# Row maxima of full attention: one transposition and one transfer for two slots, maxima four slots ahead instead of three

## The reference, cut to what matters

```python
s = jnp.einsum('bhtd,bhsd->bhts', q, k) / scale
m = jnp.max(s, axis=-1, keepdims=True)
e = jnp.exp(s - m)
num = jnp.einsum('bhts,bhsd->bhtd', e, v)
den = jnp.sum(e, axis=-1, keepdims=True) + EPS
out = (num / den).transpose(0, 2, 1, 3).reshape(B, T, H * D)
```

## Time and profile before

| what | us |
|---|---|
| median of 3 runs | 1204.31 (1196.77 to 1204.63) |
| the profiled execution | 1204.97 |
| its span, first to last instruction | 1203.2 |
| TensorE busy | 1051.9 (87%) |
| VectorE busy | 864.4 (72%) |
| ScalarE busy | 748.8 (62%) |
| mean granted TensorE clock | 0.932 |

### The profile page before, as it was taken

How to read it: one execution, slowest core, us unless ns; L and a number is a source line. 1 busy time by engine, 2 the same in 40 slices (tenths; PEclk the granted TensorE clock), 3 DMA queues, 4 the chain that set the end, 5 groups by cost and what they waited for, 6 DMA issues and landing times.

```text
span 1203.2 us, 31909 instructions
## 1 busy us (share of the span) xinstructions
PE 1051.9 (87%) x13025; PEld 484.6 (40%) x13025; DVE 864.4 (72%) x1151; ACT 748.8 (62%) x1510; POOL 90.4 (8%) x370
## 2 busy tenths in 40 slices
PE   7598999794587999899999998779898899999986
PEld 3344545442253333334444344442333334344443
DVE  3553654345554799899999944555999999999635
ACT  2422545237213389889999982231888899999921
POOL 8000100000000000000000000000000000000000
PEclk9897999888778999999999997789999999999978
DMA  3473432100006322220101000044313201001000
GB/s 96 138 211 72 98 92 74 39 1 1 0 0 189 86 64 63 55 51 18 29 19 24 24 20 10 1 124 140 71 44 72 53 18 25 22 18 30 18 15 35
DMA packets 73825, 64.97 MB, mean 54 GB/s; under 512 B 27792, under 2 KB 53648, under 8 KB 73552
## 3 DMA queue, kind: packets, MB, share of 16 engines
q1 hardware_dynamic: 73680, 62.94, 20.0%
HBM read 27.06 MB, written 35.85 MB: 52 GB/s over the span
## 4 chain that ended last, share of the span: by engine, by line
DVE 43%; PE 38%; DMA 7%; issue 4%; ACT 4%; SPq 3%; DVEq 0%; ACTq 0%
DVE nmf L1331 35%; PE wide L556 24%; PE bank L556 14%; DMA KQs<-m_dram 4%; ACT xcsq L949 2%; DVE xcsq L1148 1%; DVE res L1148 1%; SPq L378 1%; DVE nmt L1290 1%; ACT big L949 1%; SPq L309 1%; DVE big L1410 1%; SPq L299 1%; DVE x L1148 1%; DMA qf_dram<-big 1%
## 5 line engine op out<-in xcount | busy, mean ns | idle before, releaser
L1331 DVE TENSOR_REDUCE nmf<-wide 128x1 f32<-128x1024 f32 x512 | 587.3, 1204 | 40.4 <-PE wide L556 40.3
L949 ACT ACTIVATE big<-wide 128x512 f32<-128x512 f32 (+1 forms) x703 | 403.4, 601 | 81.1 <-PE wide L556 54.7
L556 PE MATMUL wide<-big,KQs 48*128 48x512 bf16 (+1 forms) x1376 | 349.4, 344 | 4.3 <-DVE nmf L1331 3.3
L556 PE MATMUL bank<-big,V 128*9 128x128 f32 x8192 | 319.9, 274 | 12.5
L556 PE MATMUL wide<-KQs,big 50*128 50x512 bf16 (+1 forms) x1035 | 266.9, 324 | 11.9 <-DMA KQs<-m_dram 10.8
L556 PEld LDWEIGHTS bank<-big,V 128*9 128x9 f32 x8192 | 176.8, 90 | 233.7 <-ACT big L949 221.7
L949 ACT ACTIVATE big<-bank 128x512 f32<-128x512 f32 (+2 forms) x473 | 233.8, 516 | 23.2 <-PE bank L556 10.6
L556 PE MATMUL bank<-KQs,big 50*128 50x512 bf16 x341 | 130.3, 382 | 6.8 <-DMA KQs<-m_dram 6.8
L556 PEld LDWEIGHTS wide<-KQs,big 50*128 50x128 bf16 x1035 | 70.6, 95 | 117.9 <-ACT big L949 56.5
L1296 DVE TENSOR_REDUCE nmw<-wide 95x4 f32<-95x512 f32 (+1 forms) x96 | 61.2, 640 | 58.9 <-PE wide L556 57.9
L949 ACT ACTIVATE xcsq<-xcsq 128x512 f32<-128x512 f32 x32 | 20.1, 630 | 124.2 <-DVE xcsq L1148 124.2
(11 more groups left out here) (175 smaller groups left out, 833.3 us busy)
## 6 DMA issues: line engine op xcount, KB each, us to landing
o_dram<-big SPq DMA_DIRECT2D x128, 64.0 KB
big<-kf_dram SPq DMA_DIRECT2D x32, 200.0 KB
kf_dram<-big SPq DMA_DIRECT2D x24, 256.0 KB, 4.2
qf_dram<-big SPq DMA_DIRECT2D x24, 256.0 KB, 4.0
KQs<-qf_dram SPq DMA_DIRECT2D x32, 192.0 KB
ow_dram<-scr SPq DMA_DIRECT2D x32, 142.5 KB
big<-kw_dram SPq DMA_DIRECT2D x16, 275.0 KB
kw_dram<-scr SPq DMA_DIRECT2D x12, 352.0 KB, 5.7
```

Of the source, the lines that this page charges most:

```text
L556: return nc.tensor.matmul(o, l, r, start=start, stop=stop, **kw)
L949: return nc.scalar.activation(o, i, f, **kw)
L1331: nc.vector.tensor_reduce(nmf[:, (s0 + i) % 4, c:c + 1], wide[:, k:k + 2, :].rearrange("p g c -> p (g c)"), AX.X, ALU.max, negate=True).th ...
```

## The change

`AHEAD` becomes 4. Slots are taken in pairs: GpSimd writes the split maxima of an even slot into columns 0 to 7 and those of the odd slot that follows into columns 8 to 15 of one `nms` buffer. VectorE transposes once per pair, after the first maximum of the slot that follows the pair. SyncE writes that block to `m_dram` once per pair and then issues two reads, one for each slot, right behind the wait for the write; it does this in even slots, for slots i + 2 and i + 3. `load_group(1)` is issued ahead of the first pair instead of after the first two slots. Windowed attention keeps its own order. `turned` itself and the semaphores stay; `nm_turned` and `nm_out` now count pairs in full attention.

```diff
--- before.py
+++ after.py
@@ -37,7 +37,7 @@
 ROW_PARTS = ((2, 1, 0, 1, 0, 0), (0, 1, 2, 0, 1, 0))
 GROUPS = 4
 SLOTS = 4 * H
-AHEAD = 3
+AHEAD = 4
 PTS = 8
 LAG = 4
 AHEAD_W = 5
@@ -68,7 +68,7 @@
         ow_dram = nc.dram_tensor("ow_dram", (B, H, 32, 4 * OW), F32).ap()
         qf_dram = nc.dram_tensor("qf_dram", (KR, H, N), BF16).ap()
         kf_dram = nc.dram_tensor("kf_dram", (KR + 2, H, N), BF16).ap()
-        m_dram = nc.dram_tensor("m_dram", (SLOTS, 32, P), BF16).ap()
+        m_dram = nc.dram_tensor("m_dram", (SLOTS // 2, 32, P), BF16).ap()
         o_dram = nc.dram_tensor("o_dram", (4, H, 4, 32, P), F32).ap()
 
         bank = [ctx.enter_context(nc.psum_tensor(f"bank{i}", [P, 512], F32)) for i in range(2)]
@@ -386,6 +386,7 @@
 
             def full_attention(layer):
                 s0 = UNITS + (layer - 1) * SLOTS
+                j0 = UNITS + (layer - 1) * SLOTS // 2
 
                 def load_group(g):
                     b, p0 = g // GROUPS, g % GROUPS * 2
@@ -404,12 +405,17 @@
                     sp.wait_ge(part_out[k], 96 * 2 * layer)
 
                 def shift(i):
-                    s = s0 + i
+                    s, j = s0 + i, j0 + i // 2
                     b, y, p, r, h = place(i)
-                    sp.wait_ge(nm_out[s % 4], 16 * (s // 4 + 1))
-                    at = S * b + 512 * y
+                    sp.wait_ge(nm_out[j % 4], 16 * (j // 4 + 1))
+                    at, o = S * b + 512 * y, 8 * (i % 2)
                     sp.dma_start(qop[r + KR:r + KR + 2, p, at:at + 512],
-                                 m_dram[i, 0:8, :].rearrange("(a c) q -> a (c q)", a=2)).then_inc(nm_in[s % 8], 16)
+                                 m_dram[i // 2, o:o + 8, :].rearrange("(a c) q -> a (c q)", a=2)).then_inc(nm_in[s % 8], 16)
+
+                def pair(i):
+                    turned(j0 + i // 2, m_dram[i // 2, :, :])
+                    shift(i)
+                    shift(i + 1)
 
                 def heads_out(i):
                     s = s0 + i
@@ -426,16 +432,11 @@
                     at = 512 * blk + P * c
                     sp.dma_start(aT[:, at:at + P], o_dram[blk, :, c, 0:D, :]).then_inc(o_in[blk], 16)
 
-                for i in range(AHEAD - 1):
-                    turned(s0 + i, m_dram[i, :, :])
-                    if i:
-                        shift(i - 1)
                 load_group(1)
+                pair(0)
                 for i in range(SLOTS):
-                    if i + AHEAD - 1 < SLOTS:
-                        turned(s0 + i + AHEAD - 1, m_dram[i + AHEAD - 1, :, :])
-                    if i + AHEAD - 2 < SLOTS:
-                        shift(i + AHEAD - 2)
+                    if i % 2 == 0 and i + 2 < SLOTS:
+                        pair(i + 2)
                     if i in LOADS:
                         load_group(LOADS[i])
                     if i:
@@ -528,11 +529,11 @@
                    [[-1, 8], [-8, H], [0, D]], 1)
             pool.drain().then_inc(moe_const, 1)
 
-            def split_shift(s, nm, rows):
+            def split_shift(s, nm, rows, j, at):
                 n = nm.shape[1]
-                first, second = nms[0:rows, s % 4, 0:n], nms[0:rows, s % 4, n:2 * n]
-                if s >= 4:
-                    pool.wait_ge(nm_turned, s - 3)
+                first, second = nms[0:rows, j % 4, at:at + n], nms[0:rows, j % 4, at + n:at + 2 * n]
+                if j >= 4:
+                    pool.wait_ge(nm_turned, j - 3)
                 pool.tensor_copy(first, nm).then_inc(nm_first, 1)
                 pool.wait_ge(nm_first, s + 1)
                 pool.tensor_tensor(second, nm, first, ALU.subtract).then_inc(nm_split, 1)
@@ -540,14 +541,14 @@
             if nst > 0:
                 for u in range(UNITS):
                     pool.wait_ge(wx_read, len(WG) * (u + 1))
-                    split_shift(u, nmw[0:QT, u % 4, :], QT)
+                    split_shift(u, nmw[0:QT, u % 4, :], QT, u, 0)
 
             for layer in (1, 2):
                 if nst > 2 * layer + 2:
                     for i in range(SLOTS):
                         n = (layer - 1) * SLOTS + i
                         pool.wait_ge(mx_read, 4 * (n + 1))
-                        split_shift(UNITS + n, nmf[:, n % 4, :], P)
+                        split_shift(UNITS + n, nmf[:, n % 4, :], P, UNITS + n // 2, 8 * (n % 2))
 
 
         @block.tensor
@@ -1283,11 +1284,11 @@
                 dve.wait_ge(g0, 5)
                 nc.vector.tensor_copy(q0o[:, :], bk(7)[:, 400:400 + B]).then_inc(g0v, 1)
 
-            def turn(s):
+            def turn(j, s):
                 dve.wait_ge(nm_split, s + 1)
-                if s >= 4:
-                    dve.wait_ge(nm_out[s % 4], 16 * (s // 4))
-                nc.vector.transpose(nmt[:, s % 4, :], nms[:, s % 4, :]).then_inc(nm_turned, 1)
+                if j >= 4:
+                    dve.wait_ge(nm_out[j % 4], 16 * (j // 4))
+                nc.vector.transpose(nmt[:, j % 4, :], nms[:, j % 4, :]).then_inc(nm_turned, 1)
 
             def windowed_attention():
                 def maximum(u, g):
@@ -1305,7 +1306,7 @@
                     for g in range(len(WG)):
                         maximum(u, g)
                         if g == 0 and u:
-                            turn(u - 1)
+                            turn(u - 1, u - 1)
                         if u == AHEAD_W + 1 and g == 0:
                             zero_out()
                     if u == 0:
@@ -1318,11 +1319,12 @@
                         zero_divide()
                     if u == H + 10:
                         reciprocal(0)
-                turn(UNITS - 1)
+                turn(UNITS - 1, UNITS - 1)
                 reciprocal(1)
 
             def full_attention(layer):
                 s0 = UNITS + (layer - 1) * SLOTS
+                j0 = UNITS + (layer - 1) * SLOTS // 2
 
                 def maximum(i, c):
                     n = 4 * ((layer - 1) * SLOTS + i) + c
@@ -1335,11 +1337,11 @@
                 for i in range(SLOTS):
                     for c in range(4):
                         maximum(i, c)
-                        if c == 0 and i:
-                            turn(s0 + i - 1)
+                        if c == 0 and i and i % 2 == 0:
+                            turn(j0 + i // 2 - 1, s0 + i - 1)
                     if i % H == 6 and i > H:
                         reciprocal(layer, i // H - 1)
-                turn(s0 + SLOTS - 1)
+                turn(j0 + SLOTS // 2 - 1, s0 + SLOTS - 1)
                 reciprocal(layer, 3)
 
             def reciprocal(layer, blk):
```

## The result

The changed kernel takes **1378.7 us** (median of 4, 1376.27 to 1382.12) against 1204.4 before (1196.77 to 1204.63): ratio 1.147, 95% interval 1.141 to 1.152. It is slower by 14.7%. The forecast was 1370, range 1330 to 1410. The profiled execution took 1376.27 us, with a span of 1374.5; before it was 1204.97 and 1203.2.

The account below looks back on a forecast made before the run. VectorE bounds now at 4.62 us per slot, TensorE at 4.56; afterwards TensorE at 6.12. Per attention 4.5 + 367.2 + 18.2 = 389.9 against 307.2; together 165.5 on 1204.97 gives 1370, range 1330 to 1410.

Parts of the forecast that it names:

- Four matmuls one behind the other: TensorE in full attention: two scores and two maxima share rows and run serially; stretch 1.53 us instead of 1.09, slot 6.12.
- The 0.09 before the values: TensorE, each stretch: 0.09 us for the step from half the rows to all, whatever the number of matmuls.
- The 0.20 taken as covered: First values of a slot wait 0.20 us for ScalarE's copy; taken as hidden after the change, otherwise the slot is 6.32.
- Weight loads: Rival: TensorE's weight loads on the same rows come into the open, stretch 1.89 us, time 1543; chance 0.05.
- Filled gaps: Rival: extra matmuls hide the 0.09 and values take 0.50, stretch 1.38 us, time 1298; chance 0.08.
- a faster kernel: Rival: score and maximum on one row range keep today's pace, slots 4.56 us, 7.5 less per attention, 1190; chance 0.04.
- VectorE, ScalarE, GpSimd: VectorE needs 4.54 us per slot, 64 fewer transpositions give nothing; ScalarE under 80% busy; GpSimd does the same work.
- SyncE's pair: SyncE's queue held 1.92 us per pair write; reads land in time, 17.6 us of waits vanish, later `heads_out` costs nothing.
- Start and end: Each full attention: one more slot of maxima first, 4.50 us; four last slots without maxima instead of three, each 4.56.
- The reciprocals: VectorE's reciprocals in full attention, 1.12 us each time, covered by TensorE's slots of 6.12.
- The sum: Both full attentions: 82.7 and 82.8 us more, together 165.5, giving 1370.

Follow-up runs that it names:

- depth4_only: Kernel before with only AHEAD 4 instead of 3, one transposition and one transfer per slot as before; 1365.6 us, ratio 1.132.
- pairs_depth3: Changed kernel with maxima three slots ahead, pairs kept; 1253.6 us, ratio 1.036 to the kernel before.
- after_recip7: Changed kernel with only VectorE's reciprocal of a finished block one slot later; 1364.4 us, ratio 1.130 to the kernel before.
- pairs_depth4_swapped: Changed kernel with heads of each pair swapped in slots 4 to 7 and 12 to 15, so slots i and i + 4 use different rows; 1213.3 us, ratio 1.003.
- depth4_swapped_recip7: Kernel before, without pairs, with AHEAD 4, heads swapped and the reciprocal one slot later; 1196.9 us, ratio 0.989.
- swapped_recip7: Changed kernel with heads swapped in slots 4 to 7 and 12 to 15 and the reciprocal one slot later; 1190.9 us, ratio 0.987 to the kernel before.

## Why the prediction was right, step by step

**Four matmuls one behind the other: right.** 1.53 us per stretch was worked out and measured, 6.12 and 6.11 per slot. The 0.09 before the values and the 0.56 of the values stayed as they were with twice the matmuls on one row range, as the earlier trace rows had promised. The 0.20 taken as covered is: all four stretches have 1.53. The Trainium skill (TensorEngine Tiling, Key Properties) says that a change of tiling mode drains the engine, which would be the 0.09; the trace agrees in so far as the step is there wherever scores or maxima give way to values, and nowhere among the four matmuls. That the drain is its cause isn't shown.

**Weight loads: the rival fell.** The timeline of TensorE's weight loads in the changed kernel, for the four matmuls from 561.05 on:

```profile
561.05 0.09 PEld L557 LDWEIGHTS wide<-KQs,big 50*128 50x128 bf16 x1 [0.22 <-ACT big L950]
561.06 0.10 PEld L557 LDWEIGHTS wide<-big,KQs 48*128 48x128 bf16 x1
561.28 0.10 PEld L557 LDWEIGHTS bank<-KQs,big 50*128 50x128 bf16 x1
561.50 0.09 PEld L557 LDWEIGHTS wide<-big,KQs 48*128 48x128 bf16 x1
```

The load at 561.06 belongs to the matmul at 561.28 and runs while the one at 561.05 streams, on the same rows. The rule that such loads don't overlap (the Trainium skill, TensorE: Matmul & The Clock Gate, Packing small matmuls) is not what this trace shows. The same section of the Trainium skill says a little earlier that a load is also pulled ahead when it goes to the background weight buffer, and the trace doesn't contradict that.

The kernel before had shown it already: the load for the second score of a stretch starts there as the first score starts, on the same rows.

```profile
547.84 0.10 PEld L556 LDWEIGHTS wide<-KQs,big 50*128 50x128 bf16 x1
```

The first score starts at 547.83 and the second at 548.05. So this rival could have been struck out instead of being given a chance.

**Filled gaps, and a faster kernel: both fell**, by the same 1.53. The condition of the faster one, four matmuls in under 0.5 us, held before (0.44) and is not met (0.88).

**VectorE, ScalarE, GpSimd: right.** VectorE was idle for 155.5 us ahead of its maxima, ScalarE's share in the slots fell to 75% (105.29 of 140 us from 560 to 700), and 64 transpositions saved bought nothing.

**SyncE's pair: right for the reads, wrong for what stands behind them.** No wait of TensorE for `m_dram` is left among the waits of the changed kernel, and the hold is 1.93 us (527.68 to 529.61) against the 1.92 of the prediction. But the prediction priced only `heads_out` behind the hold, at nothing. It left out the fetch of the sums, which came 1.44 us later than with one transfer per slot.

**Start and end: right.** The last four slots run at 4.56 as before. From the first maximum to the end of the fillers it is 23.39 us in both attentions, and was 18.97 and 19.20: 4.4 and 4.2 more, where 4.5 was taken.

**The reciprocals: the step that failed, in size.** I put them down as covered by TensorE's longer slots. That was true of their 1.12 us of work and not of what they wait for. The fourth slot brings VectorE to them one slot sooner after the fetch of the sums, and the pair makes that fetch later; four ahead alone didn't bring the wait (depth4_only), pairs at three ahead did (pairs_depth3). It cost 2.0 and 1.7 us in the changed kernel (after_recip7), and would have made my faster rival wrong by 12 us per attention (pairs_depth4_swapped). The change names nothing of that line, and yet moves it.

**The sum.** 165.5 us were predicted and 171.3 came. In the attentions, without the start, it is 158.9 instead of 156.4: the reciprocals' wait adds 3.7, the slots of 6.11 take back about 1. In the rest it is 12.3 instead of 9.0 for the two slots of maxima. The traces say where those 3.3 us lie. The start took 8.6 of the 12.3; the other 3.7 are in parts that the change doesn't touch, 0.8 ahead of the first attention, 1.4 between the two and 1.5 behind the second. The stretch ahead of the first attention alone took from 385.4 us (depth4_only) to 399.7 (depth4_swapped_recip7) in the profiled executions of these kernels, so this is within the scatter; what makes the scatter isn't shown. The same kernel, swapped_recip7, had a rest of 594.1 us in one profiled execution and 598.8 in another.

## What to carry to other kernels

Before changing how far one stage runs ahead of another, look at what stands next to what in the queue of TensorE afterwards: here a matmul of 50 rows and one of 48 took the time of one while they lay on different halves of the rows, and a distance that keeps them there is easily lost. Everything else that is hung on the running index moves with the distance as well; list each wait that follows the faster stage, and ask who feeds it and what stands ahead of that feeder in its queue. And when a bound goes away, look at the timeline of the next engine before booking the gain.

## What the runs showed of the hardware that I had not expected

Weight loads for one row range overlapped a matmul streaming on the same rows: 0.22 us from start to start for matmuls of 512 columns, the same as with different rows. A wait of 2.1 us on VectorE, 2.9 on TensorE, cost 3.7 us: matmuls behind it ran at a granted clock of 0.50 (506 to 508 us of pairs_depth4_swapped), and three stretches took 1.47 us more than at the full clock.
